# Second head group of a graph attention kernel: block transposes on VectorE and 32x32 matmuls in place of TensorE transposes

## The reference

```python
# layer 0: 8 heads of 32, masked by the adjacency matrix and the diagonal
q, k, v = proj(Wq, bq), proj(Wk, bk), proj(Wv, bv)
scores = einsum('bhqd,bhkd->bhqk', q, k) / sqrt(32)
scores = where(adj + eye > 0, scores, -inf)
out = einsum('bhqk,bhkd->bhqd', softmax(scores), v)      # then heads side by side
h = x + out @ Wo.T + bo
x1 = layernorm(h) * gamma + beta
# layer 1: one head of 256
f = x1 @ fc_w.T + fc_b
logits = (f @ q_w + q_b) + (f @ k_w + k_b).T             # masked by -1e9 * (1 - adj)
out = softmax(leaky_relu(masked, 0.01)) @ f + x1
```

## Time and profile before

| | |
|---|---|
| median of 3 runs | 985.11 us |
| the profiled execution | 985.61 us |
| its span, first to last instruction | 983.4 us |
| mean granted TensorE clock, share of full | 0.981 |
| instructions | 22056 |

### The profile page before, as it was taken

One profiled execution on the slowest core, in us unless ns is written; L12 is line 12 of the kernel. 1 busy time (PEld: TensorE's weight loads), 2 busy tenths in 40 slices (PEclk: granted clock), 3 DMA queues, 4 the chain that ended last, 5 costly groups with the idle time before them and its releaser, 6 DMA issues. The chain is left out here.

```text
span 983.4 us, 22056 instructions
## 1 busy us (share of the span) xinstructions
PE 932.2 (95%) x7432; PEld 777.8 (79%) x7432; DVE 768.7 (78%) x2012; ACT 796.1 (81%) x1900; POOL 300.5 (31%) x408
## 2 busy tenths in 40 slices
PE   4498999999999999999999999999999999999966
PEld 3276888888888888888788888878887888888755
DVE  3287987979788797978878797888879797887832
ACT  2187988989888897988889798988989898897923
POOL 0002332334333233433214243432323343232441
PEclk8699999999999999999999999999999999999988
DMA  5576856666575666657476665737666564756100
GB/s 150 85 110 149 118 141 108 130 119 99 136 116 133 108 130 129 109 126 117 123 119 133 123 129 109 118 124 116 150 111 129 108 108 130 118 120 108 44 22 22
DMA packets 74430, 112.59 MB, mean 114 GB/s; under 512 B 6736, under 2 KB 33360, under 8 KB 74320
## 3 DMA queue, kind: packets, MB, share of 16 engines
q1 hardware_dynamic: 74320, 111.18, 58.8%
HBM read 52.44 MB, written 8.39 MB: 62 GB/s over the span
## 5 line engine op out<-in xcount | busy, mean ns | idle before, releaser
L912 DVE CUSTOM_DVE_ANT_0 sm_bank<-sm_bank,masks 128x512 f32<-128x512 f32 x512 | 352.3, 698 | 124.1 <-PE sm_bank L494 121.2
L679 ACT ACTIVATE e<-sm_bank,row_min 128x512 f32<-128x512 f32 x512 | 355.3, 696 | 41.9 <-DVE row_min L912 41.9
L504 PE MATMUL et_bank<-ident,e 128*128 128x128 f32 x2048 | 307.9, 272 | 3.2 <-DVE e_t L920 1.9
L504 PEld LDWEIGHTS et_bank<-ident,e 128*128 128x128 f32 x2048 | 251.6, 140 | 42.5 <-issue 7.3
L494 PE MATMUL sm_bank<-k_stack,q_stack 96*128 96x512 f32 x512 | 248.0, 485 | 13.5 <-DMA k_stack<-kt_lo 12.7
L671 ACT COPY e_t<-et_bank 128x512 f32<-128x512 f32 x272 | 161.0, 592 | 16.1 <-PE et_bank L504 14.2
L920 DVE COPY e_t<-et_bank 128x512 f32<-128x512 f32 x240 | 164.4, 685 | 11.8 <-PE et_bank L504 10.2
L494 PEld LDWEIGHTS sm_bank<-k_stack,q_stack 96*128 96x128 f32 x512 | 97.2, 190 | 43.5 <-issue 25.5
L443 PE MATMUL o_bank<-e_t,v 128*32 128x256 f32 x2048 | 123.8, 382 | 0.0
L476 PE MATMUL shared<-feat,z 128*128 128x256 f32 x512 | 121.6, 381 | 0.8 <-ACT z L621 0.8
L679 ACT ACTIVATION_READ_ACCUMULATOR e<-sm_bank,row_min 128x1 f32 x512 | 106.9, 209 | 0.0
(11 more groups left out here) (110 smaller groups left out, 1578.9 us busy)
## 6 DMA issues: line engine op xcount, KB each, us to landing
adj_in<-in_adj SPq DMA_DIRECT2D x32, 1024.0 KB, 5.3
q_stack<-qt_hi SPq DMA_DIRECT2D x64, 256.0 KB, 7.1
k_stack<-kt_hi SPq DMA_DIRECT2D x64, 256.0 KB, 7.2
x_in<-in_x SPq DMA_DIRECT2D x16, 512.0 KB, 6.4
q_stack<-qt_lo SPq DMA_DIRECT2D x32, 256.0 KB, 7.1
k_stack<-kt_lo SPq DMA_DIRECT2D x32, 256.0 KB, 11.1
h<-in_x SPq DMA_DIRECT2D x16, 512.0 KB, 3.9
out_y<-h SPq DMA_DIRECT2D x32, 256.0 KB, 6.8
```

What stands on the lines that cost most here:

```text
L504: last = nc.tensor.transpose(et_bank[n % TURNED][:, c * P:(c + 1) * P], e[:, n % ROOM, c * P:(c + 1) * P], ident[:, :])
L679: nc.scalar.activation(e[:, k, :], sm_bank[n % SCORED][:, :], ACT.Exp, scale=-1.0, bias=row_min[:, k:k + 1], accum_out=row_sum[:, g, qt, i ...
L912: nc.vector.tensor_tensor_reduce(bank[:, :], bank[:, :], mask[b % 2][:, qt * N:(qt + 1) * N], 1.0, -LOWEST, ALU.add, ALU.min, row_min[:, k ...
```

## The change

Group 1 takes another way from `e` to the output; group 0 stays as it was. Tiles of group 1 are numbered head by head, four query blocks each.

- `turn` and `copy_turned` run for the 16 tiles of group 0 only. `DVE_COPIED` has 4 of them, ACT copies the other 12. `TURN` is 4, `ROOM` is 6.
- `turn_blocks` on DVE transposes each `e` tile of group 1 in 32x32 blocks from SBUF to SBUF, two steps after its exponential, with the keys read at a step of 4.
- `v_blocks` (8 KB per partition) holds group 1's half of `v` four times, once per quarter of the partitions. Four new DMAs per batch on SP's queue (`spread_values`, step v4) fill it from `v`.
- pv2 and pv3 become `times_v_blocks`: 128 f32 matmuls each of 32 rows, 32 columns and 128 streamed columns, in four row groups with a PSUM bank each. These four banks are both `et_bank`, `o_bank` and a shared one, and pv2 joins the queue for that shared bank.
- `o_normal` of group 1 multiplies four pieces of 128x128, one from each bank. Each bank holds the outputs of one quarter of the query rows of a block.
- `turn` of tiles 0 and 1 waits for `o_n1` of the batch before.
- `normal_rows` moves from ACT to POOL. The masks stay on DVE.
- All places in the five tables are new, and so is the order of the calls in each engine's loop.

```diff
-TURN = 3
-ROOM = 4
+TURN = 4
+ROOM = 6
+BLOCK = 2
-DVE_COPIED = (0, 3, 5, 6, 13, 14, 15, 18, 22, 24, 25, 26, 27, 28, 29)
+DVE_COPIED = (0, 3, 9, 11)
 PE_AT = {
+    "at1": 64, "pv2": 33, "rb1": 35, "pv3": 36, "op0": 40, "op1": 43, "v1": 12, "xt0": -19, "xt1": -18, "pv0": 17,
+    "ht0": 49, "ht1": 49, "fc1": 51, "fc0": 52, "kb": 52, "k0": -11, "pv1": 21, "q0": -9, "q1": -8, "rb0": 25, "k1": -5,
+    "v0": -4, "et3": 60, "et2": 60, "et1": 62, "at2": 62, "et0": 62, "at3": 62, "at0": 63}
 DVE_AT = {
+    "rc1": 32, "fin0": 64, "o_n1": 36, "h_add0": 41, "stats0": 42, "h_add1": 42, "stats1": 43, "moments": 43,
+    "x_lo0": -16, "x_lo1": -16, "rc0": 17, "h_lo0": 49, "h_lo1": 50, "q_dot1": 52, "q_dot0": 52, "l_max0": 52,
+    "l_max1": 52, "k_lo0": -11, "q_lo0": -9, "q_lo1": -8, "k_lo1": -6, "mask0": -5, "o_n0": 28, "l_recip": 61,
+    "mask1": -3, "fin1": 63}
 SP_AT = {
+    "adj": 0, "stack0": 1, "store1": 67, "adj_again": 37, "x": -24, "stack1": 9, "store0": 75, "x_again": 21, "v4": 27}
...
+        v_blocks = sb("v_blocks", [P, NT, NT, P])
+        o_quarter = [*et_bank, o_bank, bank_of["pv2"]]
...
+            def spread_values(b):
+                sp.wait_ge(act_done.sem, act_done.all("v", b))
+                sp.wait_ge(pe_done.sem, pe_done.of("pv3", b - 1))
+                for quarter in range(GH):
+                    sp.dma_start(v_blocks[quarter * DH:(quarter + 1) * DH, :, :, :], v[:, :, P:2 * P]).then_inc(v_spread.sem, 16)
...
+            def times_v_blocks(half, b):
+                pe.wait_ge(blocks_turned.sem, blocks_turned.of((half + 3) * (TILES // PAIRS) - 1, b))
+                if half == 0:
+                    pe.wait_ge(v_spread.sem, v_spread.of("v4", b))
...
+                    pe.wait_ge(dve_done.sem, dve_done.of("o_n0", b))
+                    pe.wait_ge(*bank_read("pv2", b))
...
+                for kt in range(NT):
+                    for a in range(NT):
+                        for quarter in range(GH):
+                            rows_in = slice(quarter * DH, (quarter + 1) * DH)
+                            for j in range(2):
+                                o = (2 * half + j) * DH
+                                last = nc.tensor.matmul(
+                                    o_quarter[quarter][o:o + DH, 0:P].rearrange("d (q n) -> d q n", q=NT),
+                                    v_blocks[rows_in, a, kt, o:o + DH], blocks[rows_in, j, :, kt * NT + a, :],
+                                    start=(kt == 0 and a == 0), stop=(kt == NT - 1 and a == NT - 1))
...
             def turn(u, b):
                 pe.wait_ge(exp_done.sem, exp_done.of(u, b))
+                if u < TURNED:
+                    pe.wait_ge(dve_done.sem, dve_done.of("o_n1", b - 1))
...
+                for quarter in range(GH):
+                    def part(ap):
+                        return ap[:, :].rearrange("p (q w n) -> p q w n", q=NT, w=GH)[:, :, quarter, :]
+                    last = nc.vector.tensor_tensor(part(o_raw[g]), o_quarter[quarter][:, 0:P].rearrange("p (q n) -> p q n", q=NT),
+                                                   part(recip_wide[g]), ALU.mult)
...
+            def turn_blocks(u, b):
+                dve.wait_ge(exp_done.sem, exp_done.of(u, b))
+                dve.wait_ge(pe_done.sem, pe_done.of(f"pv{u // (TILES // PAIRS) - 2}", b))
+                nc.vector.transpose(blocks_to(u), e[:, (TILES * b + u) % ROOM, :].rearrange("p (t k a) -> p t a k", t=NT, a=NT))\
+                    .then_inc(blocks_turned.sem, 1)
...
-            def normal_rows(half, b):
-                act.wait_ge(pool_done.sem, pool_done.of("shift", b))
...
+            def normal_rows(half, b):
+                pool.wait_ge(pool_done.sem, max(pool_done.of("shift", b), pool_done.of("rstd", b)))
+                for c in range(2 * half, 2 * half + 2):
+                    last = nc.gpsimd.tensor_scalar(h[b % 2][:, c, :], h[b % 2][:, c, :], rstd[:, c:c + 1], shift[:, c:c + 1],
+                                                   ALU.mult, ALU.add)
```

More of the change, by code:

```diff
@@ L124, in all @@
         return max(self.of(step, b) for step in self.place if step[:-1] == name and step[-1].isdigit())
-FILLS = [name for name, _ in steps(PE_AT) if not name.startswith("pv") and name not in ("at1", "at3")]
+FILLS = [name for name, _ in steps(PE_AT) if name not in ("pv0", "pv1", "pv3") and name not in ("at1", "at3")]
 BANK = {
-    "at2": 1, "k1": 0, "v0": 1, "op0": 0, "op1": 1, "v1": 1, "xt0": 1, "xt1": 0, "q0": 0, "ht0": 0, "ht1": 1, "k0": 1,
-    "fc0": 0, "fc1": 1, "kb": 0, "q1": 0, "et0": 0, "et1": 0, "at0": 0, "et2": 1, "et3": 0, "rb0": 1, "rb1": 1}
+    "at2": 0, "k1": 1, "v0": 0, "op0": 1, "op1": 0, "v1": 1, "xt0": 0, "xt1": 1, "q0": 1, "ht0": 0, "ht1": 1, "k0": 0,
+    "fc0": 0, "fc1": 1, "kb": 1, "q1": 0, "et0": 1, "et1": 1, "at0": 1, "pv2": 0, "et2": 0, "et3": 1, "rb0": 1, "rb1": 1}
 BANK["at1"], BANK["at3"] = BANK["at0"], BANK["at2"]
@@ L136 @@
     "fc0": ("dve", "q_dot0"), "fc1": ("dve", "q_dot1"), "kb": ("dve", "l_max"), "at0": ("dve", "fin0"),
-    "at2": ("dve", "fin1"), "rb0": ("act", "rs0"), "rb1": ("act", "rs1"), **{f"et{c}": ("act", f"et{c}") for c in range(NT)}}
+    "at2": ("dve", "fin1"), "pv2": ("dve", "o_n1"), "rb0": ("act", "rs0"), "rb1": ("act", "rs1"), **{f"et{c}": ("act", f"et{c}") for c in range(NT)}}
 def build(nc, x, adj, wq, bq, wk, bk, wv, bv, wo, bo, gamma, beta, fc_w, fc_b, q_w, q_b, k_w, k_b, out):
@@ L238, in build @@
         stacked = [Signal(sem(f"stacked{g}"), [step for step in loads if step[0] == f"stack{g}"], 16 * 6) for g in range(NG)]
+        v_spread = Signal(sem("v_spread"), [step for step in loads if step[0] == "v4"], 16 * GH)
         stored = [Signal(sem(f"stored{i}"), [step for step in loads if step[0] == f"store{i}"], 16) for i in range(2)]
@@ L445, in times_v @@
                 last.then_inc(pe_done.sem, 1)
             def turn_h(kt, b):
[L448 removed]
+                pe.wait_ge(pool_done.sem, pool_done.all("hn", b))
                 pe.wait_ge(*bank_read(f"ht{kt}", b))
@@ L508, in iteration @@
                 for s in range(TILES):
-                    if (b := due(PE_AT, "at3", s, t)) is not None:
-                        attend(3, b)
+                    if (b := due(PE_AT, "pv3", s, t)) is not None:
+                        times_v_blocks(1, b)
+                    if (b := due(PE_AT, "op0", s, t)) is not None:
+                        out_project(0, b)
+                    if (b := due(PE_AT, "op1", s, t)) is not None:
+                        out_project(1, b)
+                    if (b := due(PE_AT, "v1", s, t)) is not None:
+                        value_project(1, b)
@@ L657, in recips @@
                 copy(recip_wide[g][:, :], f"rb{g}", bank_of[f"rb{g}"][:, :], b)
-            def normal_rows(half, b):
-                act.wait_ge(pool_done.sem, pool_done.of("shift", b))
-                for c in range(2 * half, 2 * half + 2):
-                    last = nc.scalar.activation(h[b % 2][:, c, :], h[b % 2][:, c, :], ACT.Identity, bias=shift[:, c:c + 1],
-                                                scale=rstd[:, c:c + 1])
-                last.then_inc(act_done.sem, 1)
             def copy_turned(u, b):
@@ L977, in iteration @@
                         query_logits(0, b)
+                    if (b := due(DVE_AT, "mask1", s, t)) is not None:
+                        make_mask(1, b)
+                    if (b := due(DVE_AT, "fin1", s, t)) is not None:
+                        finish(1, b)
+                    u, off = ago(s, TURN)
+                    if on(t, off) and u < HALF and u in DVE_COPIED:
+                        copy_turned(u, t + off)
+                    u, off = ago(s, BLOCK)
+                    if on(t, off) and u >= HALF:
+                        turn_blocks(u, t + off)
+                    if (b := due(DVE_AT, "fin0", s, t)) is not None:
+                        finish(0, b)
+                    if (b := due(DVE_AT, "h_add1", s, t)) is not None:
+                        add_residual(1, b)
+                    if (b := due(DVE_AT, "stats1", s, t)) is not None:
+                        statistics(1, b)
+                    if (b := due(DVE_AT, "moments", s, t)) is not None:
+                        combine(b)
+                    if (b := due(DVE_AT, "x_lo1", s, t)) is not None:
+                        x_low(1, b)
                     if (b := due(DVE_AT, "l_max0", s, t)) is not None:
```

403 lines of the change are left out of this document (198 added, 205 removed), and 23 rows, old and new, of tables (ACT_AT, DVE_AT, PE_AT, POOL_AT).

## The result

The changed kernel takes **1288.61 us** (median of 4 runs, 1282.02 to 1291.36) against 985.0 (984.69 to 985.22): a ratio of 1.3073 [1.3021, 1.3125]. That is 304 us, or 19 us a batch, slower, and 233 us above 1056, the high end of the range. The profiled execution took 1291.36 us with a span of 1289.6.

A forecast was written before the change was run, and what follows sets the result against it. PE was taken as the bound, at 56.70 us a batch. Halves of 31.0 + 23.6 + 0.9, then + 1.0 - 2.0 + 0.4, gave 54.9; 985.6 - 29 + 3 = 960 us, range 938 to 1056.

The forecast's parts named there:

- The step that failed: PE, pv2 and pv3: eight tiles at work together make each call 3.65 us instead of 1.86, +3.6 us a batch.
- a list of 53.3: PE's work per batch after the change: 56.7 - 7.0 + 3.6 = 53.3 us.
- The transpose: DVE: 16 block transposes of 128x512 f32 a batch at 0.60 us each, +9.6 us.
- Case E: Rival on DVE: the block transpose takes two passes, 1.2 us, a batch near 62 us, 1070 us in all; chance 0.10.
- Turn 0 on `o_n1`: PE: turn 0 of the next batch waits for group 1's output to leave its banks, +0.9 us a batch.
- The lopsided halves and late producers: DVE's 31.0 us half and PE's 23.6 us half follow each other; fc and kb just before their readers add about 1 us.
- The parts listed for PE's batch: PE before the change: unit costs of all its matmuls and transposes, summed to 56.3 of the 56.7 us a batch.
- the removed turns: PE: 16 turns fewer per batch at 0.44 us each, -7.0 us; L504 was to have 1024 records.
- 0 for the spread of v: SP's queue: four more DMAs of 256 KB per batch are hidden, adding 0, at most 1 us.
- normalising on POOL 0: POOL: taking over `normal_rows` costs PE nothing while its chain is shorter than PE's own 5.7 us of work.
- ACT far from any bound: ACT loses 5 copies and 4 `normal_rows` a batch, falling to 44.4 us, free in any case.
- D: Rival on PE: 32x32 matmuls run four at a time, pv2 and pv3 7.0 us each, about 1050 us; chance 0.22.

The follow-up runs named there:

- the run with 8 pieces: The kernel before with each matmul of `times_v` cut in eight of 32 columns, same sums, 21768 pairs of load and matmul: 1365.06 us, 1.3869.
- the run with a quarter of the matmuls and the copy: The changed kernel with one of four key blocks multiplied in pv2 and pv3 and each block transpose replaced by a plain copy: 945.62 us, 0.9604.

## Why the prediction was wrong

**The step that failed** is "32 x 109 = 3.5, with 0.15 for the change of shape 3.65 us against 1.86: +3.6 us for both". Its question was how many tiles work together, and there it was right: rounds of eight in 0.11 us, 128 records in 1.76 us where nothing stops. What it left out is that a call is also 512 instructions, in 3.5 us: two pages that the supply did not bring faster than one in 3.7 us, and mostly far slower. In the batch shown 20.8 us pass from the first record of pv2 (396.07) to the last of pv3 (416.83), for 7.3 of forecast array time and little else. The cost comes in two parts that the sum had no term for:

- **Stops for instructions**: 145.4 us before L484 in the whole span, 9.1 us a batch. That it is the supply, the run with 8 pieces shows. That the stops are as long as they are because the data DMAs fill the engines just then is what the packets of q8 suggest; no run shows it by moving the DMAs.
- **The lower clock after them**: PE is busy 62.4 us a batch where the forecast has a list of 53.3. The 9.1 us between are mainly the stretches at 1.2 GHz: in the whole span PE is busy for 247 us at that level, before for 22. If half of the difference is what the clock costs (an estimate), that is 7.0 us a batch. With the stops gone the clock is back at 0.98 to 0.99. It also falls on what follows a stop: 108 us of that time are small matmuls, 141 are scores, turns, projections and the like.

53.3 + 9.1 + 9.1 = 71.5; the 4.9 us of idle that remain to 76.4 are mostly waits for late data, of the kind that the runs with a quarter of the matmuls show.

**The transpose**, the second term mis-sized: 0.60 forecast, 1.04 measured (0.63 with a contiguous read). Its row was right for the operation and blind to the step of 16 B, which the forecast names and does not price. With calls that don't stop it would be worth 48 us on its own (998.39 against 950.29); beside the stops it is worth 41. Case E had the size nearly right (1.2 us) for a wrong reason.

**The new waits.** Turn 0 on `o_n1`: 8.1 us in all, 0.5 a batch, forecast 0.9. The lopsided halves and late producers: a batch was to be 1.6 us over PE's list of 53.3 and is 6.1 over its list of 47.8 in the run with a quarter of the matmuls and the copy. Estimated from that run, with 5.5 us put back for full calls, the change without a single stop and with a cheap transpose would be at up to 59.4 us a batch, against 56.70: it need not have won even then. This estimate was not run; where calls lengthen beside a waiting DVE, part of the 5.5 would be hidden.

**A slip in the sum.** The parts listed for PE's batch add up to 56.0 us, not 56.3. The units thus missed 0.7 and not 0.4 us, which would put the forecast 5 us higher and changes nothing here.

**Right**: the removed turns (L549 has 1024), 0 for the spread of v (the run without it), normalising on POOL 0 (1.0001), ACT far from any bound.

**The rivals.** D said slower for four tiles at a time, 7.0 us a call. Four at a time is refuted; but a call did cost that and more (10.1 in the median). D's remark that a call over 4.5 us decides against the change was the right hinge. The rule of the Trainium skill that I set beside it ("TensorE: Matmul & The Clock Gate", starts never closer than about 25 ns) is not borne out between tiles: 128 records in 1.76 us are 13.8 ns each. No rival had the mechanism that decided. There was a trace of it before the change that I did not read: the page lists q8, and 62 packets against 14864 instructions give the page size; the forecast's own 512 records were four pages in 7.3 us, where the trace had used one in 15.6 on average.

**Left open**: whether the stops would shrink to the 1 to 2 us of the quiet pages if the loads and stacks were issued away from pv2 and pv3 (not tried; the stops over 3 us all lie where the DMA engines are full, but no run separates the two); whether the changed kernel would run free if its small matmuls were spread between the scores and turns of the whole batch (not tried: they hold both banks of `et_bank`, `o_bank` and a shared one meanwhile, which group 0 needs); and matmuls of one record each, which would halve the instructions (not tried).

## What to carry to other kernels

Price a matmul list twice, by columns streamed and by instructions: where 256 instructions (loads count) are to pass in less than about 3.5 us, PE stood still for the next page in these runs even with the DMA engines idle, and with them full a page took 5 to 11 us. A long stand costs the clock for what follows. Packing small tiles into the array multiplies instructions while it divides columns; here only calls of 64 such records, a quarter of what the result needs, ran almost without stops. Compare the places of dense PE calls with the places of the DMAs on the other queues. Let a transpose on DVE read its rows contiguously, and take the reordering into another operand.

## What was not expected of the hardware

- Pages of 16 KB of PE's program can fall behind: 6.0 us a page in the stretch shown. The kernel before uses one in 15.6 us, and the longest wait of this kind in its largest entry is 0.4 us.
- A page comes about 3.6 us after the one before in quiet stretches (past the start of the kernel no two packets of q8 begin less than 3.3 us apart in any run), and 5.4 to 11.0 us after it in the changed kernel where the DMA engines are over 0.8 busy. The mean share of a run does not tell this: with 0.59 and 0.44 the stops are the same, because the traffic beside the calls is.
- Eight 32x32 tiles in four row groups keep full rate with 128 f32 columns each: 8 records per 0.11 us at 2.4 GHz, with two records to a matmul.
- The read step of a 128x512 f32 block transpose on DVE is worth 400 ns: 1108 against 707.
